# One expert register per tile, read a tile ahead inside the down product

## What is computed

```python
probs = jax.nn.softmax(x @ Wr, axis=-1)
topk_w, topk_idx = jax.lax.top_k(probs, K)          # K = 2 of E = 8
topk_w = topk_w / jnp.sum(topk_w, axis=-1, keepdims=True)
for i in range(E):
    sel = topk_idx == i
    w_i = jnp.sum(topk_w * sel.astype(x.dtype), axis=-1, keepdims=True)
    h = jax.nn.silu(x @ Wg[i]) * (x @ Wu[i])
    e_out = h @ Wd[i]
    output = output + w_i * e_out
```

## Time and profile before

| | |
|---|---|
| median of 3 runs | 1314.36 us (1313.79 to 1315.18) |
| the profiled execution | 1314.62 us |
| its span | 1312.9 us |
| mean granted TensorE clock | 0.944 |
| TensorE busy | 1133.0 us, 86% of the span |
| VectorE busy | 877.1 us, 67% |
| ScalarE busy | 699.7 us, 53% |
| GpSimd busy | 497.0 us, 38% |

### The profile page before, as it was taken

One profiled execution on the slowest core, in us unless ns is written; L12 is line 12 of the kernel. 1 busy time (PEld: TensorE's weight loads), 2 busy tenths in 40 slices (PEclk: granted clock), 3 DMA queues, 4 the chain that ended last, 5 costly groups with the idle time before them and its releaser, 6 DMA issues. The chain is left out here.

```text
span 1312.9 us, 22452 instructions
## 1 busy us (share of the span) xinstructions
PE 1133.0 (86%) x5792; PEld 918.1 (70%) x5792; DVE 877.1 (67%) x1733; ACT 699.7 (53%) x1747; POOL 497.0 (38%) x617
## 2 busy tenths in 40 slices
PE   1099999969999978999996999996999448999997
PEld 1077877757787766777775888885788346777885
DVE  7978788786887886877888778776344545646100
ACT  7965676834757763567784466563122403433342
POOL 3074444453444453434435344351000112646432
PEclk9599999989999988999997999999899758999999
DMA  4041111114111112311111311110546506665320
GB/s 185 24 168 40 31 53 39 32 32 161 51 41 31 49 37 86 114 31 45 46 34 30 120 47 46 30 38 15 186 144 216 208 13 196 173 208 170 56 46 1
DMA packets 51715, 107.36 MB, mean 82 GB/s; under 512 B 5984, under 2 KB 26464, under 8 KB 49568
## 3 DMA queue, kind: packets, MB, share of 16 engines
q1 hardware_dynamic: 46912, 97.00, 23.0%
q0 software_dynamic: 4704, 9.18, 3.1%
HBM read 91.48 MB, written 16.52 MB: 82 GB/s over the span
## 5 line engine op out<-in xcount | busy, mean ns | idle before, releaser
L722 PE MATMUL p_proj<-w_hi,xqs 128*112 128x256 f32 (+1 forms) x512 | 177.6, 364 | 57.4 <-DVE w_lo L492 43.3
L731 PE MATMUL p_proj<-w_hi,c_hi 128*125 128x512 f32 x384 | 167.6, 437 | 19.9 <-POOL w_lo L492 18.8
L566 POOL TENSOR_TENSOR c_lo<-c_raw,c_hi 128x500 fp32r<-128x500 f32 x96 | 121.9, 1270 | 159.8 <-ACT c_hi L610 159.8
L556 POOL TENSOR_TENSOR va<-ss,epst 112x4 f32<-112x4 f32 (+2 forms) x192 | 65.4, 341 | 281.6 <-DVE ss L863 281.6
L722 PE MATMUL p_proj<-w_lo,xqs 128*112 128x256 f32 (+1 forms) x512 | 167.5, 345 | 0.0
L560 POOL TENSOR_TENSOR rs<-va,mhalf 112x4 f32<-112x4 f32 (+2 forms) x192 | 155.1, 808 | 18.0 <-POOL va L556 5.8
L731 PE MATMUL p_proj<-w_hi,c_lo 128*125 128x512 f32 x384 | 153.5, 400 | 0.0
L731 PE MATMUL p_proj<-w_lo,c_hi 128*125 128x512 f32 x384 | 153.2, 399 | 0.0
L722 PEld LDWEIGHTS p_proj<-w_hi,xqs 128*112 128x112 f32 x512 | 93.0, 182 | 74.1 <-issue 55.9
L863 DVE TENSOR_REDUCE ss<-sq 112x4 f32<-112x512 f32 (+2 forms) x192 | 96.3, 504 | 53.7 <-ACT sq L631 44.9
L659 ACT ACTIVATE pcross<-p_cross,nmax 112x375 f32<-112x375 f32 x128 | 73.2, 575 | 104.5 <-DVE nmax L892 104.2
(11 more groups left out here) (232 smaller groups left out, 2758.1 us busy)
## 6 DMA issues: line engine op xcount, KB each, us to landing
c_raw<-in_ctxT SPq DMA_DIRECT2D x96, 250.0 KB, 2.6
shared<-in_w_in SPq DMA_DIRECT2D x16, 1024.0 KB, 9.8
shared<-in_wproj SPq DMA_DIRECT2D x32, 256.0 KB, 3.0
raw_g<-in_Wg SPq DMA_DIRECT2D x8, 1024.0 KB
raw_u<-in_Wu SPq DMA_DIRECT2D x8, 1024.0 KB, 7.4
raw_d<-in_Wd SPq DMA_DIRECT2D x8, 1024.0 KB, 5.6
cat_scratch<-cat SPq DMA_DIRECT2D x32, 224.0 KB, 1.9
shared<-cat_scratch SPq DMA_DIRECT2D x2, 1792.0 KB, 8.2
```

The lines of the kernel that those rows point to most:

```text
L556: pool.tensor_tensor(va[0:rows, lo:hi], ss[0:rows, lo:hi], epst[0:rows, lo:hi], ALU.add).then_inc(va_done, 1)
L566: pool.tensor_tensor(flat(c_lo[:, k, :, :]), flat(c_raw[:, k, :, :]), flat(c_hi[:, k, :, :]).bitcast(F32), ALU.subtract).then_inc(cl_done, 1)
L722: m = pe.matmul(bank[0:T, o:o + w], xqs[:, n, k, :], (w_hi, w_lo)[i % 2][:, k, lo:lo + w], start=(i == 0), stop=(i == 2 * KB - 1))
L731: m = pe.matmul(bank[0:CT, :], a[:, ch, k, :], w[:, k, CKX:CV], start=(i == 0), stop=(i == 3 * KB - 1))
```

## The change

The table shrinks to 21 + 8 entries: the slot offsets are gone. One value_load a tile reads the expert's number plus one, and the offset is worked out from it on TensorE's sequencer as (split & 1) * 4. For this the slots are swapped: an expert of even number has the second slot. The load for tile i + 1 stands between the two halves of the down product of tile i - 1, behind rest_of_rows(i + 1); the load for tile 0 stands ahead of turn_rows(0). VectorE no longer makes an integer copy of the tile's expert nor the offset.

```diff
     def slot(self, half, e, n):
-        return flat(half[n][:, e % 2 * KB:e % 2 * KB + KB, :])
+        at = (e + 1) % 2 * KB
+        return flat(half[n][:, at:at + KB, :])
...
-    of_tile_u = sb(c, "of_tile_u", [P, TI], U32)
-    tab = sb(c, "tab", [P, 2 * TI + EX], U32)
+    tab = sb(c, "tab", [P, TI + EX], U32)
...
         def weights_of(i):
-            return (pe.value_load(tab[0:1, i:i + 1], min_val=0, max_val=KB),
-                    pe.value_load(tab[0:1, TI + i:TI + i + 1], min_val=1, max_val=EX))
-
+            split = pe.value_load(tab[0:1, i:i + 1], min_val=1, max_val=EX)
+            return pe.snap((split & 1) * KB, min_val=0, max_val=KB), split
+
+        at, split = {}, {}
+        at[0], split[0] = weights_of(0)
         turn_rows(0)
         rest_of_rows(0)
-        at = {}
         for i in range(TI):
-            at[i], split = weights_of(i)
             pe.wait_ge(xl_done, i + 1)
-            pe.wait_ge(l_done[0], split)
+            pe.wait_ge(l_done[0], split[i])
...
             if i + 1 < TI:
                 rest_of_rows(i + 1)
+                at[i + 1], split[i + 1] = weights_of(i + 1)
             if i >= 1:
                 products(pd, hh[:, :], hl[:, :], 2, at.pop(i - 1), (2, 3)).then_inc(dn_rdy, 1)
...
-            link(v.tensor_copy(of_tile_u[:, :], of_tile[:, :]))
-            v.tensor_scalar(tab[:, 0:TI], of_tile_u[:, :], 1, 2, ALU.bitwise_and, ALU.logical_shift_left)
             link(v.tensor_scalar(of_tile[:, :], of_tile[:, :], 1.0, None, ALU.add))
-            v.tensor_copy(tab[:, TI:2 * TI], of_tile[:, :])
-            v.tensor_copy(tab[:, 2 * TI:], end[:, :]).then_inc(tab_done, 1)
+            v.tensor_copy(tab[:, 0:TI], of_tile[:, :])
+            v.tensor_copy(tab[:, TI:], end[:, :]).then_inc(tab_done, 1)
...
-                done = v.value_load(tab[0:1, 2 * TI + e - 2:2 * TI + e - 1], min_val=1, max_val=TI)
+                done = v.value_load(tab[0:1, TI + e - 2:TI + e - 1], min_val=1, max_val=TI)
```

More of the change, by code:

```diff
@@ L1517, in _ @@
                 pe.wait_ge(up_done, i)
-            pe.wait_ge(l_done[1], split)
+            pe.wait_ge(l_done[1], split[i])
             products(pu, xh[:, i % 2, :], xl[:, i % 2, :], 1, at[i], range(KB)).then_inc(u_rdy, 1)
-            pe.wait_ge(l_done[2], split)
+            pe.wait_ge(l_done[2], split.pop(i))
             if i + 1 < TI:
```

## The result

The changed kernel takes 1305.67 us, the median of 12 runs, against 1312.68 us for 12 runs of the kernel before. The ratio is 0.9948, with a 95% interval of 0.9937 to 0.9960: 6.8 us faster. The medians themselves are 7.0 us apart. Of the 4.8 us between the forecast time and the measured one, 1.7 us are the baseline (1314.36 from 3 runs, 1312.68 from 12); 3.1 us (2.9 by the ratio) are the argument's own error, and these are what follows.

A forecast was written before the change was run, and what follows sets the result against it. TensorE's turns were taken as the bound, with 7.7 us lost from y at 1106.91 to y at 1290.12 in every other turn, behind hf. -8.8 - 0.3 + 4.4 + 0.8 = -3.9 us gave 1310.5 us, range 1307.5 to 1315.5.

The forecast's parts named there:

- The gap behind hf: Before the gate product in slow turns: moving the register loads from behind hf removes TensorE's idle gap, -8.8 us.
- the five waits of 0.18 for hf: Before p_h in five slow turns: TensorE's 0.18 us waits for GpSimd's hf would be swallowed and go.
- The table: VectorE's chain ahead of the experts' loop: two steps, the CAST and the shift, go, -0.3 us.
- Tile 0's load: Ahead of the first p_x: the load lies about under 0.93 us of matmuls, 0 with 0.2 us either way.
- The stall in the middle of pd: Before the down product's second half: the moved load makes weights late, 0.23 us in each of 19 turns, +4.4 us.
- the 0.12 that come for free: Middle of the down product: a late weight load skips waiting for the matmul before it, giving back 0.12 us.
- 0.1 for the & and: Middle of the down product: the offset's arithmetic was taken to run right behind the load, as fused steps, 0.1 us.
- 0.11 for the address step: Middle of the down product: the address step of pd itself was counted on top of the load, 0.11 us.
- The adds: GpSimd's adds to the output in slow pairs: shorter pairs make them wait for the previous add's landing, +0.8 us.
- TensorE feels all of it but 0.05: Slow pairs: nearly all the lateness of GpSimd's add would reach TensorE, all but 0.05 us.
- the hidden load: Rival, middle of the down product: load fits the sequencer's lead, stall under 0.1; about -6 us, 1308.4 us; chance 0.14.
- second check: Middle of the down product: a bounds check on the computed offset, 0.3 us, making the stall 0.55 to 0.6 a turn.

The follow-up runs named there:

- the doubled load: Changed kernel with two loads of the same table entry in the middle of the down product: 1319.76 us, ratio 1.0055 to the kernel before.
- the last experiment: Changed kernel with load ahead of the wait for xh, gather before add, tile 0's load behind the first transposes: 1303.25 us, ratio 0.9931 to the kernel before.

## Why the prediction was wrong

The mechanism was right in every part but the last term; the argument was off by 3 us because two terms of the sum had the wrong size, both in the same direction. That the time also left the range owes 1.7 us to the baseline: counted from the 12 runs of the kernel before, the range would end at 1305.8, and 1305.67 lies at that edge.

- **The gap behind hf (-8.8).** Right as to what goes: the gap vanishes in every slow turn, and the first one with it. The first one gave 1.10 where 1.1 was taken: 0.87 of waiting, and 3.06 against 2.83 for the gate product behind it. The -0.98 of the table is what is left of it after the 0.07 of the lower clock and the stall in the down product of tile 0. But the sum took the five waits of 0.18 for hf as gone with it. They stayed: p_h still starts behind hf (1123.10), and the pair of 19.77 is 0.17 longer than two turns of 9.80.
- **The table (-0.3).** 0.29. Right.
- **Tile 0's load (0, 0.2 either way).** +0.13, and the last experiment gives it back.
- **The stall in the middle of pd (+4.4).** This is the step that failed, by its size: "a stall of 0.23 us in each of 19 turns". The method was sound. The sequencer's lead, the 0.65 of a load (0.64 by the doubled load) and the 0.12 that come for free all measured as read. Wrong was what I laid on top: 0.1 for the & and *, which are issued ahead of the next gate product, and 0.11 for the address step, where 0.06 lie between its start and the weight load. So the load is 0.20 late and not 0.35 in the common turn, and past the free 0.12 the turn is 9.80: 0.05 over the 9.75 of before, or 0.09 over the 9.71 that the turn takes with no stall at all. Two of the seven quiet turns have 0.35 and 9.94, which is the stall of 0.23 as forecast over 9.71. Seven quiet turns grew by 0.57 us, 0.08 each. All eighteen turns together are 2.03 us over 18 x 9.75, the 0.85 or so of hf waits among them, so the stall came to about 1.2 net where 4.1 were laid on these turns.
- **The adds (+0.8).** Nothing. The landings did hold up adds in more turns, as argued; the add at 1135.47 has the DMA as its releaser and was 0.8 late. But a late add cost nothing, since its end is tied to the end of VectorE's subtraction of the down weights (1.47 us behind it, on time or late) and not to its own start. The step "TensorE feels all of it but 0.05" was wrong.

So -8.8 - 0.3 + 4.4 + 0.8 = -3.9 turned into -6.9: the stall about 3 us smaller, the adds 0.8 smaller, and the waits for hf 0.85 still there. The last of these offsets the others, by chance and not by the argument. Of the rivals, the hidden load came nearest in time with -6, but its mechanism isn't what happened, as the stall is there. Its experiment, the load ahead of the wait for xh, has 67.99 us for the seven turns and the changed kernel 68.86. The "second check" never appeared. One sum slipped: a stall from 0.17 to 0.28 and a DMA term from 0.3 to 1.2 make 1308.9 to 1311.8, not 1309.3 to 1311.7; it changes nothing here.

The rule of the Trainium skill that was weighed (DMA: Bandwidth & Descriptors, Latency and other measured facts: a floor of about 600 ns for a tensor_load) doesn't fit this case: the load at 1219.7 took 303 ns, and a whole value_load with check and assertion 0.64.

## What to carry to other kernels

An in-order sequencer has a lead over its engine that its last wait caps. Before placing a register load, measure that lead at each candidate place, as the time from the last released wait to the next engine instruction that is due. One line earlier, ahead of the wait and not behind it, made the difference between a stall in every turn and none, and made the count of registers irrelevant in the loop. Price an expression on a register where its value is first used.

When an engine's chain is late, ask whether its parts end with their own duration or with something else. An instruction whose end doesn't move with its start is held by another engine. Ask then which instruction of that engine it started in, and not only which one ended just ahead of it; then reorder what stands behind it.

## What the hardware showed that I had not expected

- GpSimd's indirect DMAs take 1.6 and 1.0 us with VectorE quiet and 3.6 and 2.9 in the turns in which VectorE splits weights. In all ten profiles an add that starts during a two-input operation of VectorE on 128 x 2048 ends 1.44 to 1.52 us after the end of that operation, whatever its start. GpSimd's tensor_tensor grows from 1.30 to 3.38 us when it starts just behind such an operation's start, and VectorE's own subtraction from 2.29 to 3.57 when GpSimd's tensor_tensor starts just behind its start. That a shared resource is behind it is inferred from these times; no run isolates it.
- The granted clock fell in the last eight matmuls of the program in three of ten profiles and made the last turn 1.5 us longer. Moving the load ahead of the wait for xh had gained 1.39 us in eighteen turns.
- The turn without a stall is 9.71 us in the kernels with one load, or with loads ahead of the wait for xh, but was 9.75 before, although no gap stood in it. Most of the 0.04 us shows in the gate product (2.82 against 2.79 for 12 matmuls in the chain). One load fewer on the way to it brings them back; how they arise stays open.
- Two of the seven quiet turns have 0.15 us more between the same instructions of the sequencer, at the same tiles in three profiles. It goes with the place in the program; why is open as well.
